# A second-order attention and expert kernel: two block sums left to TensorE, and the row turning, the router and the row load at other places in the batch

## The chip, the cores and the metric

The kernel runs on one core of one Trainium2 chip. The metric is the time of one execution on the device in microseconds (us). The median of three runs before the change is 1181.84 us, from 1178.0 to 1183.53.

## The reference

A layer of attention and a layer of experts, on 8 batches of 512 rows of 256 values, all fp32. Attention uses the second-order Taylor form of the exponential, so a weight is the polynomial 1 + s/4 + s²/32 of the score s; "enc" keys and values come from the first 128 rows of a batch and are seen by all rows.

```python
A_qk = jnp.tril(jnp.einsum('bhnd,bhmd->bhnm', q_f, k_f))      # q_f, k_f: Taylor features
y1 = jnp.einsum('bhnm,bhme->bhne', A_qk, v)
y2 = jnp.einsum('bhnm,bhme->bhne', jnp.einsum('bhnd,bhmd->bhnm', q_f, k_enc_f), v_enc)
k_state = k_enc_f.sum(axis=2, keepdims=True) + jnp.cumsum(k_f, axis=2)
z = 1.0 / ((q_f * k_state).sum(axis=-1) + EPS)                # the denominators
x = _layernorm(x + ((y1 + y2) * z[..., None]) ... @ Wout.T)
# then: 8 experts, each row goes to its best one (router logits x @ wr + br),
# gelu(x @ w1 + b1) @ w2 + b2, times a gate, added to x, and a second layernorm
```

## The kernel before

**Stages.** `attention` runs from the start to about 797 us, `route` (sorting the rows by expert) to about 828 us, and `run_experts` (39 tiles of 128 rows) to the end at 1178.5 us. Only `attention` and its handing over to `route` are touched.

**Pairs, gaps and units.** Attention works through 8 batches b, each of 8 pairs of heads p (n = 8b + p counts them). A pair has four units u: unit 0 is the enc block (512 columns of queries), unit 1 the key block 0 (512), unit 2 the key blocks 3 and 1 (128 + 384), unit 3 the key block 2 (256). A batch has 32 gaps g, one for each unit of each pair: g = 4p + u. In gap g TensorE (PE) makes the scores of unit u of the next pair (`scores(n + 1, u)`, into the PSUM tiles `slot`), weighs the values with unit u of this pair (`weigh(n, u)`, into `osum`), after unit 3 adds up the denominators (`denominators(n)`, into `den`), and then does what a table gives this gap: one *piece*. All pieces go through one PSUM tile, `piece`, so each piece waits (`take_piece`) until another engine has read the one before it. Pieces are the projections of values (`V_LATE_AT` for this batch's second half, `V_EARLY_AT` for the next batch's first half), the projections of queries and keys for the next batch (`QK_AT`), the output projection of the last batch (`OUT_AT`), the turning of its normalised rows (`TURN_AT`) and its router logits (`ROUTER_AT`). The numbers in these tables, `piece_numbers()` and the loops of each engine are all that sets the order; each engine's program is in fixed order.

**Weights.** ScalarE (ACT) squares the scores of a unit into `w`, VectorE (DVE) masks and adds a half (`finish_weights`, L508 and L511). GpSimd (POOL) sums the four key blocks and the enc block of a pair into `wsum`, 512 columns for each of two heads, in five instructions (`add_blocks`: L343, L344, L347, L350, L354), and `denominators(n)` multiplies `wsum` with a column of ones at row p: four matmuls of 256 columns on four 32-column tiles of the array (head s and half c of the queries each have one). `onehot` holds that column. `den` collects 8 pairs; ACT copies it, DVE inverts it at gap 1 of the next batch, SyncE's queue (SP) writes it to `inv_rows` in DRAM (`store_inverse`) and loads it back spread over partitions (`load_inverse`), and DVE multiplies it in (`normalise`, gaps of `NORM_AT`, L520).

**Operands.** Queries and keys of the next batch are split in a high part (ACT, `high_qk`) and a low part (DVE, `low_qk`, L500), written to DRAM by SP (`send(b + 1, m)`: 8 heads for each m, two stores each of `qh`, `ql`, `kh`, `kl`) and gathered back (`gather(b, g)`: `kop` and `qop` of two pairs). `gather(b + 1, 1)`, for pairs 2 and 3, stands in SP's queue behind all of `send(b + 1, 1)`, and so behind the pieces `QK_AT` numbers 3 and 4; PE needs it for the scores of pair 2, at gap 4 of batch b + 1. The projection of queries and keys needs `xl`, the low part of the next batch's input, which DVE makes at gap `XL_GAP` (L492).

**Rows.** `y` holds a batch's input rows (`load_rows`, 512 KB), to which DVE adds the output projection (`residual`), then statistics (`moments`), POOL's `deviation` and DVE's `centre` (L560). SP stores the result, PE turns it (`turn_rows`, L710), ACT copies it to `yT`, PE makes the 8 logits of each row (`router`, L717), and DVE adds the bias (`logits_of`, L565). The next rows may be loaded only when these are turned.

## Time and profile before

| | |
|---|---|
| median of three runs | 1181.84 us |
| the profiled execution: its time, its span | 1180.28 us, 1178.5 us |
| PE busy, of the span | 1063.4 us, 90% |
| DVE, POOL, ACT busy | 634.1, 613.0, 508.0 us |
| last denominators of batches 0 to 7 end at | 117.6, 216.1, 309.1, 402.7, 496.5, 591.5, 684.2, 763.5 us |
| mean granted TensorE clock | 0.95 |

A batch of attention takes 93 to 98 us, the first 117.6 and the last, which projects nothing for a successor, 79.3. The profile is of one execution. Busy time of PE is modelled: matmuls overlap in the pipeline. So stage costs are best read as the distance from the start of one group to the start of the next, and idle time as what stands in square brackets behind a group: how long, and what ended it.

### The profile page before, as it was taken

What the parts mean: (1) busy time and instruction counts of PE and PEld (TensorE: products, weight loads), DVE (VectorE), ACT (ScalarE), POOL (GpSimd) and SP (SyncE); (2) the same over time, 40 slices, a digit from 0 to 9 for tenths busy, and PEclk for the clock granted to TensorE, in tenths of its full rate; (3) what the DMA queues carried; (4) which work ended last, traced back from release to release, by engine and by line L of the source; (5) the groups of instructions that cost most, each with busy time, mean ns of one, the idle gap of its engine ahead of it and who ended that gap; (6) DMA issues with size and microseconds to landing.
All of it is one profiled execution on the core that took longest, in us unless ns stands there. A gap on an engine that the chain in (4) does not pass through costs nothing. (4 is left out here: it accounts for less than half of the span.)

```text
span 1178.5 us, 16833 instructions
## 1 busy us (share of the span) xinstructions
PE 1063.4 (90%) x5296; PEld 621.4 (53%) x5297; DVE 634.1 (54%) x963; ACT 508.0 (43%) x891; POOL 613.0 (52%) x635
## 2 busy tenths in 40 slices
PE   5699899989989989989999998883679999999994
PEld 4344355445445445436545544463357766766763
DVE  5396864683693683585476468447123343333332
ACT  2466644654654663653664464400123233233231
POOL 1397654664673674665576567500134544444442
PEclk9799989999999999999999998995789999999998
DMA  5733631741651552453273261104821011101010
GB/s 208 260 102 106 201 125 64 234 151 41 201 178 69 176 176 97 141 181 126 70 217 122 84 208 59 36 1 197 349 116 33 29 31 34 33 29 33 30 30 1
DMA packets 54111, 134.91 MB, mean 114 GB/s; under 512 B 5854, under 2 KB 10176, under 8 KB 51746
## 3 DMA queue, kind: packets, MB, share of 16 engines
q1 hardware_dynamic: 50306, 124.81, 31.5%
q0 software_dynamic: 3744, 9.31, 2.5%
q8 instruction: 35, 0.57, 0.2%
q14 instruction: 26, 0.21, 0.1%
HBM read 87.73 MB, written 47.29 MB: 115 GB/s over the span
## 5 line engine op out<-in xcount | busy, mean ns | idle before, releaser
L384 ACT ACTIVATE w<-slot 128x1024 f32<-128x1024 f32 (+1 forms) x256 | 231.2, 916 | 176.3 <-PE slot L730 176.1
L751 PE MATMUL osum<-w,values 128*64 128x512 f32 (+3 forms) x1280 | 253.6, 492 | 5.7 <-DVE w L511 5.7
L508 DVE SCALAR_TENSOR_TENSOR w<-w,mask 128x256 f32<-128x256 f32 (+1 forms) x192 | 175.8, 916 | 150.8 <-ACT w L384 138.0
L343 POOL TENSOR_TENSOR wsum<-w 128x512 f32<-128x512 f32 x64 | 95.7, 1496 | 222.7 <-DVE w L511 222.7
L511 DVE TENSOR_SCALAR w<-w 128x768 f32<-128x768 f32 (+2 forms) x192 | 189.4, 986 | 0.0
L347 POOL TENSOR_TENSOR wsum<-wsum,w 128x768 f32<-128x768 f32 x64 | 124.8, 1951 | 60.0 <-DVE w L511 58.2
L1161 ACT ACTIVATE active<-upT,b 128x128 f32<-128x128 f32 x312 | 84.9, 383 | 158.3 <-PE upT L1239 158.3
L1215 PE MATMUL down<-w,active 128*128 x624 | 144.1, 385 | 2.5 <-ACT active L1161 2.5
L1227 PE MATMUL up<-w,rowsT 128*128 x312 | 143.1, 602 | 0.7 <-ACT rowsT L1150 0.7
L730 PE MATMUL slot<-qop,kop 64*128 64x512 f32 (+3 forms) x640 | 126.6, 426 | 9.8 <-issue 7.2
L1215 PEld LDWEIGHTS down<-w,active 128*128 128x128 f32 x624 | 117.5, 193 | 18.6 <-issue 3.8
L730 PEld LDWEIGHTS slot<-qop,kop 64*128 64x128 f32 x640 | 56.2, 188 | 124.3 <-issue 110.5
L674 PE MATMUL piece<-wo,att 128*128 128x256 f32 x448 | 105.5, 389 | 5.7 <-DVE kl L500 5.3
L674 PEld LDWEIGHTS piece<-wo,att 128*128 128x128 f32 x448 | 83.8, 192 | 34.2 <-ACT values L397 9.7
L1192 DVE COPY inner<-up 128x1024 f32<-128x1024 f32 x39 | 47.8, 1225 | 91.7 <-PE up L1227 91.7
L751 PEld LDWEIGHTS osum<-w,values 128*64 128x64 f32 x1280 | 65.4, 136 | 58.5 <-issue 43.3
L344 POOL TENSOR_TENSOR wsum<-w 128x512 f32<-128x512 f32 x64 | 94.1, 1470 | 0.0
L354 POOL TENSOR_TENSOR wsum<-wsum,w 128x512 f32<-128x512 f32 x64 | 86.9, 1358 | 12.2 <-DVE w L511 7.7
L1227 PEld LDWEIGHTS up<-w,rowsT 128*128 128x128 f32 x312 | 57.2, 193 | 58.7 <-issue 58.6
L1175 DVE TENSOR_TENSOR result<-down,b 128x256 f32<-128x256 f32 x39 | 16.6, 425 | 113.5 <-PE down L1215 111.0
L397 ACT ACTIVATE values<-piece 128x512 f32<-128x512 f32 x75 | 44.9, 598 | 75.6 <-PE piece L627 75.5
L389 ACT ACTIVATE w<-w 128x1024 f32<-128x1024 f32 x64 | 67.8, 1060 | 2.0
(187 smaller groups left out, 1210.7 us busy)
## 6 DMA issues: line engine op xcount, KB each, us to landing
kop<-k_rows SPq DMA_DIRECT2D x32, 640.0 KB, 5.8
qop<-q_rows SPq DMA_DIRECT2D x32, 512.0 KB, 7.5
w<-in_w SPq DMA_DIRECT2D x16, 1024.0 KB, 9.3
inv<-inv_rows SPq DMA_DIRECT2D x56, 256.0 KB, 4.5
k_rows<-kh SPq DMA_DIRECT2D x32, 320.0 KB
k_rows<-kl SPq DMA_DIRECT2D x32, 320.0 KB
q_rows<-qh SPq DMA_DIRECT2D x32, 256.0 KB
q_rows<-ql SPq DMA_DIRECT2D x32, 256.0 KB
```

The costliest lines, as they stand in the source:

```text
L343: pool.tensor_tensor(dst[:, 0, :], src[:, 0, 0:N], src[:, 0, N:2 * N], ALU.add)
L344: pool.tensor_tensor(dst[:, 1, :], src[:, 1, 0:N], src[:, 1, N:2 * N], ALU.add).then_inc(wsummed, 1)
L347: pool.tensor_tensor(dst[:, :, P:N], dst[:, :, P:N], src[:, :, 2 * N + P:3 * N], ALU.add).then_inc(wsummed, 1)
L354: pool.tensor_tensor(dst[:, :, 2 * P:N], dst[:, :, 2 * P:N], src[:, :, 3 * N:WIDTH], ALU.add).then_inc(wsummed, 1)
L384: act.activation(w[:, n % 2, :, at:at + cols], slot[u % 2][:, :, 0:cols], ACT.Square, bias=HALF_ROOT).then_inc(squared, 1)
L508: dve.scalar_tensor_tensor(src[:, :, 0:cut], src[:, :, 0:cut], 0.5, mask[:, 0:cut].unsqueeze(1).to_broadcast([P, 2, cut]), ALU.add, ALU.mu ...
L511: dve.tensor_scalar(src[:, :, cut:], src[:, :, cut:], 0.5, None, ALU.add).then_inc(w_ready, 1)
L674: last = pe.matmul(piece[:, 0:D], att[:, (b * PAIRS + p) % ATT, t * P:t * P + P], wo[:, p, :], start=(p == 0), stop=(p == PAIRS - 1))
L730: last = pe.matmul(slot[u % 2][:, s, col:col + N - q0], kop[HD * s:HD * s + HD, n % RING, j * P:j * P + P], qop[HD * s:HD * s + HD, n % RI ...
L751: last = pe.matmul(osum[n % 2][HD * s:HD * s + HD, q0:N], values[:, j, h * HD:h * HD + HD], w[:, n % 2, s, at:at + N - q0], start=(u == 0) ...
L1215: last = pe.matmul(down[k % 2][:, :], active[:, k % 2, c, :], w2[:, bass.ds(e, 1), c, :].rearrange("p o d -> p (o d)"), start=(c == 0), st ...
L1227: last = pe.matmul(up[:, h * 512:(h + 1) * 512], rowsT[:, k % 2, c, :], w1[:, bass.ds(e, 1), c, h * 512:(h + 1) * 512].rearrange("p o d -> ...
```

## The change

- **Denominators.** POOL makes three of its five sums: enc + block 0, and block 1 added to the last 384 columns. Block 2 (256 columns of queries) and the first part of unit 2 (block 3, 128 columns) aren't summed; `denominators` multiplies them straight out of `w`. It becomes 12 matmuls for a pair instead of 4: four of 256, four of 128 and four of 64 columns. For this the halves c are 64 of every 128 columns, not 256 of 512, so `store_inverse` writes runs of 64 values and `spread_inverse` writes strided columns.
- **`square`** waits for the denominators of pair n - 2 in place of its weighing and sums.
- **Turning and router** of batch b's rows move from gaps 26, 28, 30 of batch b + 1 to gaps 7, 9, 10 of batch b + 2. Batch 6 keeps the old places in batch 7.
- **Logits**: ACT copies them out of `piece` and signals it free; DVE adds the bias in SBUF.
- **Tables**: `QK_AT` moves from gaps 10, 12, 14, 25, 27 to 11, 13, 15, 27, 29; `OUT_AT` and `V_EARLY_AT` one gap later, and with them the moments, the deviation and `centre`; one piece of `V_LATE_AT` from gap 5 to 4.
- **Rows**: SP loads `y` behind `gather(b, 3)` in the next batch's queue in place of behind `gather(b + 1, 1)`.

```diff
-RING, ATT, INV = 4, 14, 4
-V_LATE_AT = {0: 0, 1: 1, 3: 2, 5: 3, 6: 4}
-QK_AT = {10: 0, 12: 1, 14: 2, 25: 3, 27: 4}
-OUT_AT = {15: 0, 17: 1, 19: 2, 21: 3}
-V_EARLY_AT = {16: 0, 18: 1, 20: 2, 22: 3, 24: 4}
-TURN_AT, ROUTER_AT = {26: 0, 28: 1}, 30
+RING, ATT, INV = 4, 13, 4
+V_LATE_AT = {0: 0, 1: 1, 3: 2, 4: 3, 6: 4}
+QK_AT = {11: 0, 13: 1, 15: 2, 27: 3, 29: 4}
+OUT_AT = {16: 0, 18: 1, 20: 2, 22: 3}
+V_EARLY_AT = {17: 0, 19: 1, 21: 2, 23: 3, 25: 4}
 XH_GAP, XL_GAP = 7, 8
-NORM_AT = {4: 0, 5: 1, 6: 2, 7: 3, 9: 4, 10: 5, 12: 6, 13: 7}
-INVERT_GAP, MOMENTS_GAP, CENTRE_GAP, RSTD_GAP = 1, 22, 24, 23
+NORM_AT = {4: 0, 5: 1, 6: 2, 7: 3, 9: 4, 10: 5, 11: 6, 13: 7}
+INVERT_GAP, MOMENTS_GAP, CENTRE_GAP, RSTD_GAP = 1, 23, 25, 24
...
+def turned_at(b, g):
+
+    if b >= 2 and g in (7, 9, 10):
+        return [(b - 2,) + {7: ("turn", 0), 9: ("turn", 1), 10: ("router", 0)}[g]]
+    if b == B - 1 and g in (26, 28, 30):
+        return [(b - 1,) + {26: ("turn", 0), 28: ("turn", 1), 30: ("router", 0)}[g]]
+    return []
...
-                        sp.dma_start(inv_rows[PAIRS * s:PAIRS * s + PAIRS, QH * c:QH * c + QH],
-                                     den_sb[at:at + PAIRS, :]).then_inc(inv_out, 16)
+                        rows = inv_rows[PAIRS * s:PAIRS * s + PAIRS, :].rearrange("h (t c n) -> h t c n", c=2, n=64)
+                        sp.dma_start(rows[:, :, c, :], den_sb[at:at + PAIRS, :]).then_inc(inv_out, 16)
...
                 gather(b, 3)
+                if b > 1:
+                    load_rows(b - 1)
                 if b + 1 < B:
                     send(b + 1, 0)
...
                     send(b + 1, 1)
                     gather(b + 1, 1)
-                if b > 0:
-                    load_rows(b)
+            load_rows(B - 1)
...
                 elif u == 2:
-                    pool.wait_ge(wsummed, 4 * n + 1)
+                    pool.wait_ge(wsummed, 2 * n + 1)
                     pool.tensor_tensor(dst[:, :, P:N], dst[:, :, P:N], src[:, :, 2 * N + P:3 * N],
-                                       ALU.add).then_inc(wsummed, 1)
-                    pool.wait_ge(wsummed, 4 * n + 2)
-                    pool.tensor_tensor(dst[:, :, 3 * P:N], dst[:, :, 3 * P:N], src[:, :, 2 * N:2 * N + P],
-                                       ALU.add).then_inc(wsummed, 1)
-                else:
-                    pool.wait_ge(wsummed, 4 * n + 3)
-                    pool.tensor_tensor(dst[:, :, 2 * P:N], dst[:, :, 2 * P:N], src[:, :, 3 * N:WIDTH],
                                        ALU.add).then_inc(wsummed, 1)
...
                 if n >= 2:
-                    act.wait_ge(weighed, UNITS * (n - 2) + u + 1)
-                    act.wait_ge(wsummed, 4 * (n - 1))
+                    act.wait_ge(den_full, n - 1)
...
+            def copy_logits(b):
+                act.wait_ge(piece_full, nth(b, "router", 0) + 1)
+                act.activation(logits[:, bass.ts(b, NT), :], piece[:, 0:NT * E].rearrange("p (t e) -> p t e", e=E),
+                               ACT.Copy).then_inc(raw_copied, 1)
+                act.wait_ge(raw_copied, b + 1)
+                act.sem_inc(piece_read, 1)
...
             def logits_of(b):
-                dve.wait_ge(piece_full, nth(b, "router", 0) + 1)
-                dve.tensor_tensor(logits[:, bass.ts(b, NT), :], piece[:, 0:NT * E].rearrange("p (t e) -> p t e", e=E),
-                                  br[:, :].unsqueeze(1).to_broadcast([P, NT, E]), ALU.add).then_inc(piece_read, 1)
+                dve.wait_ge(raw_copied, b + 1)
+                own = logits[:, bass.ts(b, NT), :]
+                dve.tensor_tensor(own, own, br[:, :].unsqueeze(1).to_broadcast([P, NT, E]), ALU.add)
...
             def denominators(n):
                 b, p = n // PAIRS, n % PAIRS
-                pe.wait_ge(wsummed, 4 * n + 4)
+                pe.wait_ge(wsummed, 2 * n + 2)
...
+                summands = [(0, lambda s: wsum[:, n % 2, s, :]), (2, lambda s: w[:, n % 2, s, 3 * N:WIDTH]),
+                            (3, lambda s: w[:, n % 2, s, 2 * N:2 * N + P])]
+                for k, (t0, src) in enumerate(summands):
+                    for s in range(2):
+                        for c in range(2):
+                            at = 32 * (2 * s + c)
+                            last = pe.matmul(den[at:at + 32, 64 * t0:QH], onehot[:, 31 - p:63 - p],
+                                             src(s).rearrange("p (t c n) -> p t c n", c=2, n=64)[:, :, c, :],
+                                             start=(p == 0 and k == 0), stop=(p == PAIRS - 1 and k == 2),
+                                             tile_position=(0, at), skip_group_check=True)
```

PE before, in batch 3, from unit 2 of gap 10 into gap 12 (`piece<-xh,wqk_h` begins a query or key piece, `slot` is scores, `osum` weighing):

```order
L730 MATMUL slot<-qop,kop 128x128 x2
L730 MATMUL slot<-qop,kop 128x384 x2
L751 MATMUL osum<-w,values 64x128 x2
L751 MATMUL osum<-w,values 64x384 x2
L627 MATMUL piece<-xh,wqk_h 128x512 x2
L627 MATMUL piece<-xl,wqk_h 128x512 x2
L627 MATMUL piece<-xh,wqk_l 128x512 x2
L730 MATMUL slot<-qop,kop 128x256 x2
L751 MATMUL osum<-w,values 64x256 x2
L764 MATMUL den<-wsum,onehot 32x256 x4
L730 MATMUL slot<-qop,kop 128x512 x2
```

PE with the change, at the same place, from unit 2 of gap 10 to the query piece (`piece<-ident,y` would be a turned block, `piece<-wr,yT` is the router):

```order
L722 MATMUL piece<-ident,y 128x128 x4
L742 MATMUL slot<-qop,kop 128x128 x2
L742 MATMUL slot<-qop,kop 128x384 x2
L763 MATMUL osum<-w,values 64x128 x2
L763 MATMUL osum<-w,values 64x384 x2
L729 MATMUL piece<-wr,yT 128x8 x8
L742 MATMUL slot<-qop,kop 128x256 x2
L763 MATMUL osum<-w,values 64x256 x2
L779 MATMUL den<-wsum,onehot 32x256 x4
L779 MATMUL den<-w,onehot 32x128 x4
L779 MATMUL den<-w,onehot 32x64 x4
L638 MATMUL piece<-xh,wqk_h 128x512 x2
```

The query piece stood in gap 10, straight behind the weighing of unit 2; now the router's matmuls stand there, and the query piece comes behind unit 3 and a denominator group of three kinds of matmul.

POOL before, the sums of one pair, and then with the change:

```order
L343 TENSOR_TENSOR wsum<-w 128x512
L344 TENSOR_TENSOR wsum<-w 128x512
L347 TENSOR_TENSOR wsum<-wsum,w 128x2x384
L350 TENSOR_TENSOR wsum<-wsum,w 128x2x128
L354 TENSOR_TENSOR wsum<-wsum,w 128x2x256
```

```order
L350 TENSOR_TENSOR wsum<-w 128x512
L351 TENSOR_TENSOR wsum<-w 128x512
L354 TENSOR_TENSOR wsum<-wsum,w 128x2x384
```

The sums over 2x128 and 2x256 columns are gone.

SP before, between the last operands gathered ahead for a batch and the next batch's own gathers (`inv_rows`: the inverted denominators going out, `inv`: coming back):

```order
L227 DMA kop<-k_rows 128x2x640
L230 DMA qop<-q_rows 128x2x512
L194 DMA y<-in_x 128x1024
L188 DMA xT<-in_xT 128x1024
L242 DMA inv_rows<-den_sb 8x256 x4
L253 DMA inv<-inv_rows 64x1024 x4
L227 DMA kop<-k_rows 128x2x640
L230 DMA qop<-q_rows 128x2x512
L253 DMA inv<-inv_rows 64x1024 x4
L227 DMA kop<-k_rows 128x2x640
```

SP with the change, at the same place, up to the load of the rows:

```order
L233 DMA kop<-k_rows 128x2x640
L236 DMA qop<-q_rows 128x2x512
L194 DMA xT<-in_xT 128x1024
L249 DMA inv_rows<-den_sb 32x1x64 x4
L259 DMA inv<-inv_rows 64x1024 x4
L233 DMA kop<-k_rows 128x2x640
L236 DMA qop<-q_rows 128x2x512
L259 DMA inv<-inv_rows 64x1024 x4
L233 DMA kop<-k_rows 128x2x640
L236 DMA qop<-q_rows 128x2x512
L200 DMA y<-in_x 128x1024
```

The load of `y` no longer follows the gather of `kop` and `qop` that is issued ahead for the next batch; it follows that batch's last gather.

## Rows read from the trace of the kernel before

**Rows 1.** Windows, core 0: stretch, length, busy time by engine (instructions), granted clock, DMA.

```profile
117.50:763.50 646.00, 613.84 (x3344) 321.04 (x3340) 403.85 (x551) 343.21 (x453) 400.28 (x294) 0.98 0.42 135
117.50:216.10 98.60, 92.62 (x494) 48.49 (x490) 61.74 (x82) 50.68 (x67) 59.29 (x44) 0.95 0.42 135
216.10:309.10 93.00, 88.54 (x494) 46.90 (x490) 58.02 (x81) 50.53 (x67) 57.30 (x43) 1.00 0.45 144
```

**Rows 2.** Waits over the whole span: total us, times, longest.

```profile
POOL wsum L343 <- DVE w L511: 222.7, 63, 32.9
...
PE piece L627 <- DVE xl L492: 19.3, 7, 4.9
```

**Rows 3.** PE's timeline, batch 3: start, us, group, [idle before, releaser].

```profile
336.17 0.70 PE L627 MATMUL piece<-xh,wqk_h 128*128 128x512 f32 x2 [3.02 <-DVE xl L492]
...
350.42 3.72 PE L674 MATMUL piece<-wo,att 128*128 128x256 f32 x16 [0.75 <-DVE kl L500]
```

**Rows 4.** Windows again: the stretch behind batch 3's wait for `xl`.

```profile
337.00:340.50 3.50, 3.50 (x18) 1.25 (x16) 3.50 (x4) 1.11 (x2) 3.23 (x2) 0.52 0.16 35
```

**Rows 5.** PE's timeline at full clock, end of batch 2 into batch 3.

```profile
302.15 0.66 PE L710 MATMUL piece<-ident,y 128*128 128x128 f32 x4
...
304.18 0.55 PE L730 MATMUL slot<-qop,kop 64*128 64x128 f32 x4
...
305.68 1.95 PE L717 MATMUL piece<-wr,yT 128*128 128x8 f32 x16
307.56 0.39 PE L730 MATMUL slot<-qop,kop 64*128 64x256 f32 x2
307.87 0.65 PE L751 MATMUL osum<-w,values 128*64 128x256 f32 x4
308.46 0.64 PE L764 MATMUL den<-wsum,onehot 128*32 128x256 f32 x8
309.03 0.50 PE L730 MATMUL slot<-qop,kop 64*128 64x512 f32 x2
309.45 1.08 PE L751 MATMUL osum<-w,values 128*64 128x512 f32 x4
310.46 0.73 PE L627 MATMUL piece<-wv_h,xh 128*128 128x512 f32 x2
```

**Rows 6.** POOL's and DVE's timelines there; POOL's two lines, ns min/median/max.

```profile
309.59 1.83 POOL L347 TENSOR_TENSOR wsum<-wsum,w 128x768 f32<-128x768 f32 x1
...
309.65 1.92 DVE L511 TENSOR_SCALAR w<-w 128x256 f32<-128x256 f32 x1
...
L350 POOL TENSOR_TENSOR wsum<-wsum,w x64: 725/788/1794, 43.0 to 760.7; 128x256 f32<-128x256 f32 x64
...
L354 POOL TENSOR_TENSOR wsum<-wsum,w x64: 1262/1280/1662, 43.8 to 761.5; 128x512 f32<-128x512 f32 x64
```

**Rows 7.** PE's and SP's timelines, batch 3 into 4; DMA issues there, us to landing.

```profile
389.17 0.56 PE L730 MATMUL slot<-qop,kop 64*128 64x128 f32 x4
...
401.24 1.44 SPq L230 DMA_DIRECT2D qop<-q_rows  x1
...
qop<-q_rows SPq DMA_DIRECT2D x1, 512.0 KB, 8.8
...
413.31 0.51 PE L730 MATMUL slot<-qop,kop 64*128 64x512 f32 x2
```

**Rows 8.** PE's timeline, batch 0 into 1.

```profile
107.15 0.55 PE L730 MATMUL slot<-qop,kop 64*128 64x128 f32 x4
...
128.65 0.50 PE L730 MATMUL slot<-qop,kop 64*128 64x512 f32 x2 [0.39 <-DMA qop<-q_rows]
```

**Rows 9.** PE's timeline, the last batch.

```profile
716.91 1.12 PE L751 MATMUL osum<-w,values 128*64 128x256 f32 x4 [1.88 <-DVE w L511]
...
754.49 0.63 PE L710 MATMUL piece<-ident,y 128*128 128x128 f32 x4 [2.37 <-DVE y L560]
```

**Rows 10.** ACT's timeline: a copy of 256 columns out of PSUM.

```profile
309.16 0.39 ACT L436 ACTIVATE den_sb<-den 128x256 f32<-128x256 f32 x1 [0.58 <-PE den L764]
```

More of the change, by code:

```diff
@@ L456, in _ @@
                         copy_values(b + 1, 0, V_EARLY_AT[g - 1])
[L457 to L458 removed]
+                    for owner, kind, k in turned_at(b, g - 1):
+                        if kind == "turn":
+                            copy_turned(owner, k)
+                        else:
+                            copy_logits(owner)
                     if b + 1 < B and g == XH_GAP:
@@ L594, in _ @@
                         residual(b - 1, OUT_AT[g - 1])
-                    if b > 0 and g - 1 == ROUTER_AT:
-                        logits_of(b - 1)
+                    for owner, kind, _ in turned_at(b, g - 1):
+                        if kind == "router":
+                            logits_of(owner)
                     if n < B * PAIRS and u > 0:
@@ L791, in _ @@
                         project_values(b + 1, 0, V_EARLY_AT[g])
-                    if b > 0 and g in TURN_AT:
-                        turn_rows(b - 1, TURN_AT[g])
-                    if b > 0 and g == ROUTER_AT:
-                        router(b - 1)
+                    for owner, kind, k in turned_at(b, g):
+                        if kind == "turn":
+                            turn_rows(owner, k)
+                        else:
+                            router(owner)
             spread_inverse(0)
```

22 lines of the change are left out of this document (7 added, 15 removed).

## The prediction

> **What bounds the kernel now.** I read the windows first [rows 1]. From the end of batch 0's denominators to the end of batch 7's PE is busy 613.84 of 646.00 us, so it idles 32.2 us, and the granted clock there is 0.98: some 13 us went by the half clock (0.02 x 646). DVE, ACT and POOL are busy 404, 343 and 400 us. PE is the bound of attention, and the others count only where PE waits for them. So I read the waits next [rows 2]: POOL's 222.7 us of waiting for DVE cost nothing, PE's 19.3 us in seven waits for `xl` do. The timeline shows the place [rows 3]: gap 10, where the first query piece starts; later in the batch PE waits a second time, 0.75 us, for a key piece's low part. Behind the first of these the clock stands at 0.52, about 1.2 GHz, for 3.5 us [rows 4]; batch 1, where the wait was longest, has a mean of 0.95 and batch 2 has 1.00 [rows 1].
>
> Why is DVE late? At 309.59 POOL starts a sum and ends at 311.42; DVE's addition of a half, started at 309.65, ends at 311.57 [rows 6]. It does nothing while POOL's instruction runs. So POOL's sums cost DVE time, and through it PE.
>
> **Denominators on PE.** Before, a pair's group takes 309.03 - 308.46 = 0.57 us [rows 5]. Added are 192 columns on each of the four array tiles, in eight matmuls (16 instructions, since an fp32 matmul is two). The price of a column: weighing 256 columns of two heads takes 308.46 - 307.87 = 0.59 us, 512 columns 310.46 - 309.45 = 1.01 us, so 0.42 / 256 = 1.64 ns per column where the tiles work beside each other [rows 5]. Lower bound: 192 x 1.64 ns = 0.32 us. Upper bound: each narrower kind also pays the fixed 0.57 - 0.42 = 0.15 us of a group again, 0.62 us. Between them: a weight load of 32 columns belongs to each instruction, and 64 columns give it little cover. The router's matmuls of 8 columns show what a load costs by itself: (307.56 - 305.68) / 16 = 0.117 us for 128 columns [rows 5], so four of 32, one after another, need about as long as a step of 128 columns streams. Taking the 64-column steps as dear as the 128-column ones gives 256 x 1.64 = 0.42, rounded up to 0.43 us, my value. For 64 pairs: **+27.5 us** (20.5 to 40). All of it is on the path, since PE is the bound.
>
> The Trainium skill, page TensorEngine Tiling (Array Packing), section Key Properties, says that different tiles can load weights and multiply in parallel. By it the loads of the four tiles would hide even under 64 columns, and the sum would have 20.5 in place of 27.5; no row here shows tiles under such short streams. It is a rival below.
>
> **POOL's two sums gone.** They take 0.79 and 1.28 us a pair [rows 6], 2.07 us, and nearly all of it is room for DVE in the stretch where DVE is late, three pairs from gap 4 on: some 6 us by gap 16.
>
> **Turning, router and tables.** In batches 2 to 7 two turned blocks (about 0.6 us each; 0.66 us busy) and the router (1.88 us) now stand before the first query piece, and that piece is behind gap 11 instead of 10 (scores, weighing and denominators of unit 3, 309.03 - 307.56 = 1.47 us, plus 0.43) [rows 5]. PE reaches it 3.1 + 1.9 + 0.4 (the earlier pair's denominators) = 5.4 us later, against a wait of 3.02 us [rows 3]. Batch 1 has no turned rows yet and gains only 2.3 us by this, with 2 us or more from POOL's relief, against the longest wait, 4.9 us [rows 2]. So the seven waits go: **-19.3 us**. Of the remaining idle time, 32.2 - 18.2 (six of these waits) = 14.0 us, 2.4 us is a turned block waiting for `centre` in the last batch, and 0.4 us a wait for operands [rows 8, 9]; the rest, 11.2 us, are waits for DVE's low parts and, in the last batch, for weights and sums (1.88 us is the longest) [rows 9]. With 6 us more room for DVE they go: **-11.2 us**. With them goes the half clock, **-13 us**. What would be late next is ACT: it must copy the second turned block within gap 10, where PE scores and weighs for 1.50 us (304.18 to 305.68) [rows 5] and a copy of twice the 256 columns that take 0.39 us [rows 10] fits; I take nothing.
>
> Moving the work costs nothing: batch 1 loses 3.1 us and batch 7 gains it. In batch 7 `centre` is a gap later, but before it waited for POOL, which now is free sooner; the 2.37 us stay.
>
> **The operands for pairs 2 and 3.** Here is the price. Pieces 3 and 4 of `QK_AT` go two gaps later, and the router and turned blocks that stood behind them are gone. Before, from the end of piece 3 (389.17) to the scores that need the gather (413.31) PE worked 24.1 us; the gather's last load, issued at 401.24, landed 8.8 us later, at 410.0, 20.9 us after piece 3 [rows 7]. It had 3.3 us to spare. Now PE's time is 24.1 less two gaps (1.50 for unit 2, 1.47 for unit 3), less two blocks and a router (3.1), plus two denominator groups (0.86): 19.0 us. A chain of 20.9 is 1.9 us late, and PE waits with nothing else in its queue. The rows' load, 512 KB, used to follow the gather and its packets ran beside it; now it is gone from there. That may give back up to 1 us. Against it stands batch 0: no rows' load behind the gather, no turned blocks, and PE did wait, at 128.65, 21.5 us after piece 3 (107.15) [rows 8]. I take 2.5 us after batch 0, 1.2 us for the next five and 0.5 for the last: **+9 us** (0 to 17.5), and **+1.5 us** for a clock that falls once.
>
> **SP's queue.** The rows' load is now between `gather(b, 3)` at gap 11 and the first store of queries, where SP waits for that piece anyhow; it has five gaps, at 1.4 us and a piece each, to land, against the 8.8 us of a load of the same size [rows 7]. `store_inverse` writes runs of 256 bytes instead of 1 KB; a tenth or two later, with DVE's room as cover.
>
> **Logits.** Only the last batch's are on the path, at the head of `route`: an ACT copy, below the 0.39 us of a 256-column copy [rows 10], and one more hand-over, **+0.4 us**.
>
> **Sum.** 27.5 - 19.3 - 11.2 - 13 + 9 + 1.5 + 0.4 = -5.1 us. The profiled execution took 1180.28 us, which gives 1175.2; it lies 1.6 us under the median of the runs, 1181.84, which would give 1176.7. I say **1175 us**.
>
> **The rivals.**
> *The narrow matmuls cost only their columns* (the page's rule): 0.32 a pair, 7 us less, 1168 us. For it: the gap of unit 2, with 128 and 384 columns, takes 1.50 us, and one with 512 in one block 310.46 - 309.03 = 1.43 us, so the split costs 0.07 us [rows 5]. Chance 0.13.
> *The operands land in time*: without the rows' packets the chain is under 19 us, and 10.5 us are saved: 1164.5 us. Against it: batch 0. Chance 0.15.
> *The operands are late as after batch 0, and the clock falls each time*: seven waits of 2.5 us (17.5) and seven stretches of 3.4 us at half clock (7 x 1.7 = 12) instead of 10.5: 1175 + 19 = **1194 us**, slower than before. For it: a wait of 3.02 us did bring the half clock [rows 3, 4]. It makes the kernel slower from some 2.2 us a batch, clock included: 10.5 + 5.1 = 15.6 over seven. Chance 0.12.
> *The upper price of the denominators*: 0.62 a pair, 12 us more, 1187 us. Chance 0.08.
> *The waits for DVE stay*: POOL's sums were not what held it, because DVE starts late at gap 4, for the inverses from DRAM, which now come in smaller runs. Half of the 30.5 us idle and some clock less half of what is saved would give 1175 + 10 to 15, some 1187 us. Against it: PE itself comes 5.4 us later. Chance 0.10.
>
> **How the numbers follow.** My sum, 1169 to 1181, has 0.42. A measurement of this kernel can tell 0.5%, about 6 us: below 1175.9 is faster, above 1187.7 slower. Faster: the two cheap cases (0.28) and over half of my own (0.23), 0.51. Slower: 0.12 and a part of the two at 1187, 0.14. Within: 0.35. The range, 1162 to 1187, leaves out the slow case and the two cheap ones together.
>
> **What the changed profile would show.** The denominator group 1.0 us from its start to the next group (0.89 and 1.19 are the rivals). No PE wait for `xl` or for DVE's low parts. A wait of PE's scores for `qop` at gap 4 of each batch, 1 to 2.5 us. DVE's 256-column addition less often near 1.9 us. Batches 2 to 6 of about 92 to 93 us, batch 1 of about 91. Batches over 95 us, or a PE wait at gap 11, would make me wrong.

## The result and the profile after

The changed kernel took 1196.18 us (median of 4 runs, 1193.95 to 1201.36), the kernel before beside it 1182.22 (4 runs, 1178.0 to 1183.53): ratio 1.0113, 95% interval 1.0073 to 1.0153. It is slower, by 14 us, where 1175 was forecast with a range up to 1187. The profiled execution is the longest of the four, 1201.36 us with a span of 1199.6. Its span is 21.1 us longer than the 1178.5 of before, so the sizes below are those of that execution, and the medians differ by less. In every ratio of this document the runs over 1.5% above the fastest of their kernel are left out; three of the twelve of experiment 8 are such runs, its profiled one among them.

The same windows as in [rows 1], from the end of batch 0's denominators to the end of batch 7's and then three batches:

```profile
116.40:784.50 668.10, 640.34 (x4240) 351.82 (x4236) 371.89 (x551) 346.63 (x460) 280.40 (x181) 0.96 0.41 131
116.40:213.90 97.50, 92.08 (x598) 49.80 (x594) 52.51 (x80) 49.80 (x65) 39.65 (x27) 0.95 0.40 130
213.90:310.30 96.40, 92.67 (x622) 51.26 (x618) 54.29 (x81) 50.98 (x68) 40.22 (x27) 0.98 0.43 137
501.20:600.50 99.30, 95.50 (x618) 52.59 (x618) 54.76 (x81) 51.09 (x68) 40.17 (x27) 0.95 0.43 133
```

The stretch went from 646.00 to 668.10 us, and it holds the whole loss. PE is busy 26.5 us longer (640.34 against 613.84) and idles 27.8 us in place of 32.2. So of the 30 us of waits that were to go most did go, and another wait took their place. The waits of PE say which, beside [rows 2]:

```profile
PE slot L742 <- DMA qop<-q_rows: 17.5, 7, 3.3
...
PE piece L722 <- DVE y L570: 9.2, 2, 5.3
...
PE piece L638 <- DVE ql L510: 6.4, 4, 3.6
```

The scores wait for the query operands after every batch, seven times and 17.5 us in all. PE's timeline at the end of batch 2 and into batch 3, which answers to [rows 5] and [rows 7]:

```profile
300.89 0.73 PE L638 MATMUL piece<-xh,wqk_h 128*128 128x512 f32 x2
...
302.49 0.51 PE L742 MATMUL slot<-qop,kop 64*128 64x512 f32 x2
...
309.36 0.64 PE L779 MATMUL den<-wsum,onehot 128*32 128x256 f32 x8
309.81 0.51 PE L779 MATMUL den<-w,onehot 128*32 128x128 f32 x16
310.26 0.50 PE L742 MATMUL slot<-qop,kop 64*128 64x512 f32 x2
...
320.66 0.63 PE L638 MATMUL piece<-wv_h,xl 128*128 128x512 f32 x2
323.95 0.76 PE L742 MATMUL slot<-qop,kop 64*128 64x512 f32 x2 [2.65 <-DMA qop<-q_rows]
```

Key piece 3 starts at 300.89 and is over at 302.49. The scores that need its gather could begin at 323.95 - 2.65 = 321.30, and begin at 323.95. A pair's denominators take 310.26 - 309.36 = 0.90 us. The window right behind the wait, in the columns of [rows 4]:

```profile
324.10:327.40 3.30, 3.30 (x8) 1.16 (x9) 0.00 (x0) 2.56 (x3) 0.00 (x0) 0.50 0.05 17
```

The clock granted there is 0.50, that is 1.2 GHz, after a wait in which PE did nothing. A stretch at 0.50 follows each of the seven waits, 30.7 us in all, and at half rate that is 15 us lost. In batches 5 and 6, the two of 99 us, there is one more, and no wait stands before it. It comes straight behind the router, whose 16 matmuls are of 8 columns each:

```profile
533.22 1.95 PE L729 MATMUL piece<-wr,yT 128*128 128x8 f32 x16
```
```profile
535.70:539.00 3.30, 3.30 (x31) 1.87 (x28) 3.30 (x3) 0.47 (x1) 2.94 (x2) 0.50 0.67 200
634.70:638.00 3.30, 3.30 (x30) 1.83 (x27) 3.30 (x3) 0.50 (x1) 2.94 (x2) 0.50 0.73 210
```

SP's issues around the wait in batch 3 (start, how long the issue took), and the first multiplication by an inverse on DVE:

```profile
301.38 0.36 SPq L264 DMA_DIRECT2D attention_rows<-y  x1
303.28 1.22 SPq L216 DMA_DIRECT2D q_rows<-qh  x2
...
309.06 2.69 SPq L225 DMA_DIRECT2D k_rows<-kl  x2
311.85 1.69 SPq L233 DMA_DIRECT2D kop<-k_rows  x1
313.59 1.41 SPq L236 DMA_DIRECT2D qop<-q_rows  x1
315.04 1.06 SPq L194 DMA_DIRECT2D xT<-in_xT  x1
317.53 2.81 SPq L249 DMA_DIRECT2D inv_rows<-den_sb  x4
325.96 2.41 SPq L259 DMA_DIRECT2D inv<-inv_rows  x4
```
```profile
330.70 0.69 DVE L530 TENSOR_TENSOR att<-att,inv 128x512 f32<-128x512 f32 x1 [9.20 <-DMA inv<-inv_rows]
```

Three things stand here. The load of the query operands is issued at 313.59 and lands when the wait ends, 10.4 us later. The four stores of the inverses take 2.81 us to issue, and the first load behind them follows 8.4 us after they began. In the kernel before these were 1.30 and 3.25 us in the same batch:

```profile
316.30 1.30 SPq L242 DMA_DIRECT2D inv_rows<-den_sb  x4
319.55 2.42 SPq L253 DMA_DIRECT2D inv<-inv_rows  x4
```

So there are two suspects for the loss, late operands and late inverses.

### The profile page after: what moved, and what is told of

It reads as the page before. It is cut to its first block and busy times, and to the rows that moved or that the text cites. A ratio compares the mean times of both kernels' runs of the same rounds, so it can differ in the third digit from the quotient of the medians.

```text
span 1199.6 us, 18706 instructions
## 1 busy us (share of the span) xinstructions
PE 1090.7 (91%) x6320; PEld 654.8 (55%) x6321; DVE 596.8 (50%) x963; ACT 511.1 (43%) x899; POOL 477.3 (40%) x507
## 5 line engine op out<-in xcount | busy, mean ns | idle before, releaser
L763 PE MATMUL osum<-w,values 128*64 128x512 f32 (+3 forms) x1280 | 258.0, 500 | 0.4 <-DVE w L521 0.3
L518 DVE SCALAR_TENSOR_TENSOR w<-w,mask 128x256 f32<-128x256 f32 (+1 forms) x192 | 141.5, 737 | 154.8 <-ACT w L383 143.2
L521 DVE TENSOR_SCALAR w<-w 128x768 f32<-128x768 f32 (+2 forms) x192 | 170.7, 889 | 0.0
L742 PE MATMUL slot<-qop,kop 64*128 64x512 f32 (+3 forms) x640 | 127.3, 428 | 26.9 <-DMA qop<-q_rows 17.5
L530 DVE TENSOR_TENSOR att<-att,inv 128x512 f32<-128x512 f32 x56 | 38.2, 682 | 63.4 <-DMA inv<-inv_rows 63.4
```

The costliest lines, as they stand in the source:

```text
L518: dve.scalar_tensor_tensor(src[:, :, 0:cut], src[:, :, 0:cut], 0.5, mask[:, 0:cut].unsqueeze(1).to_broadcast([P, 2, cut]), ALU.add, ALU.mu ...
L521: dve.tensor_scalar(src[:, :, cut:], src[:, :, cut:], 0.5, None, ALU.add).then_inc(w_ready, 1)
L742: last = pe.matmul(slot[u % 2][:, s, col:col + N - q0], kop[HD * s:HD * s + HD, n % RING, j * P:j * P + P], qop[HD * s:HD * s + HD, n % RI ...
L763: last = pe.matmul(osum[n % 2][HD * s:HD * s + HD, q0:N], values[:, j, h * HD:h * HD + HD], w[:, n % 2, s, at:at + N - q0], start=(u == 0) ...
```

## The experiments

The lengths are windows from the end of batch 0's denominators to the end of batch 7's, as in [rows 1]. PE's idle time is the length less its busy time; the waits for operands are those of the scores for `qop` at gap 4. Ratios are to the kernel before, run on the same chip as the kernel in question (17 runs of it in the second and third group of kernels, 11 in the first, experiments 1 to 4), with 95% intervals. A profile is one execution, and it need not be the median one.

| kernel | median us | ratio | window | PE busy | PE idle | operands' waits | clock |
|---|---|---|---|---|---|---|---|
| before | 1182.2 | 1 | 646.0 | 613.8 | 32.2 | 0.4 | 0.98 |
| changed | 1196.2 | 1.0113 (1.0073 to 1.0153) | 668.1 | 640.3 | 27.8 | 17.5 | 0.96 |
| pieces 3, 4 earlier | 1193.7 | 1.0114 (1.0075 to 1.0152) | 663.1 | 637.7 | 25.4 | 15.6 | 0.97 |
| denominators alone | 1170.2 | 0.9908 (0.9878 to 0.9939) | 641.3 | 625.0 | 16.3 | none | 0.99 |
| all but the denominators | 1205.1 | 1.0227 (1.0185 to 1.0269) | 670.3 | 624.0 | 46.3 | 18.0 | 0.96 |
| layout alone | 1191.4 | 1.0094 (1.0065 to 1.0124) | 656.0 | 621.7 | 34.3 | 0.3 | 0.96 |
| pieces earlier, y behind | 1166.6 | 0.9874 (0.9844 to 0.9905) | 632.7 | 623.9 | 8.8 | none | 0.99 |
| late half back | 1173.5 | 0.9910 (0.9874 to 0.9946) | 638.6 | 625.9 | 12.7 | none | 0.99 |
| late half back, pieces late | 1190.6 | 1.0055 (1.0026 to 1.0083) | 660.4 | 635.4 | 25.0 | 14.2 | 0.97 |
| denominators, 1 KB runs | 1162.4 | 0.9833 (0.9801 to 0.9864) | 632.8 | 623.0 | 9.8 | none | 0.99 |
| pieces, y behind, 1 KB runs | 1166.1 | 0.9876 (0.9845 to 0.9908) | 631.7 | 623.9 | 7.8 | none | 0.99 |
| y behind alone | 1201.1 | 1.0170 (1.0128 to 1.0211) | 668.8 | 640.6 | 28.2 | 12.8 | 0.96 |
| changed, 1 KB runs | 1199.2 | 1.0147 (1.0116 to 1.0178) | 666.6 | 638.3 | 28.3 | 17.1 | 0.97 |
| pieces, y behind, old denominators | 1177.0 | 0.9977 (0.9954 to 0.9999) | 636.3 | 613.9 | 22.4 | none | 0.98 |

**1. The second send's pieces earlier.** The changed kernel with one line different:

```
-QK_AT = {11: 0, 13: 1, 15: 2, 27: 3, 29: 4}
+QK_AT = {11: 0, 13: 1, 15: 2, 24: 3, 26: 4}
```

> The changed kernel, with the key pieces 3 and 4 of the next batch behind gaps 24 and 26 in place of 27 and 29 (three gaps, about 4.7 us of TensorE's work, earlier), and nothing else. Theory A: the loss is made by late operands. In the changed kernel TensorE waits seven times, 17.5 us in all, for the DMA of the query operands at gap 4, and behind each wait stands a stretch of 3.4 us or more at half clock. Three gaps are more than the longest of these waits (3.3 us), so all seven go, and the clock stretches behind them: 1196 less 17.5 less 7 x 1.7 = 12 gives 1167 us, or up to 1176 if some of the clock is lost elsewhere; mean clock of batches 1 to 7 at 0.97 or more. Rival B: DVE is late for the inverses, whose stores now go in runs of 256 bytes; then the wait moves from the operands to DVE's values and the time stays above 1185 us. Rival C: the pieces, three gaps earlier, themselves wait for DVE's low parts (kl, 0.5 us now), and half of the gain is given back: 1180 us.

1193.7 us, where 1167 to 1176 was expected: a miss. Six waits for the operands remained, 15.6 us. But this run shows where the three gaps went. DVE and SP at the end of batch 2:

```profile
293.66 0.69 DVE L510 SCALAR_TENSOR_TENSOR ql<-piece,qh 128x512 fp32r<-128x512 f32 x1 [5.19 <-ACT qh L408]
...
295.38 3.31 DVE L570 TENSOR_SCALAR y<-y,mv,rstd 128x256 f32<-128x256 f32 x4
```
```profile
298.72 0.36 SPq L264 DMA_DIRECT2D attention_rows<-y  x1
299.19 1.21 SPq L216 DMA_DIRECT2D q_rows<-qh  x2
...
311.37 1.57 SPq L236 DMA_DIRECT2D qop<-q_rows  x1
```

DVE had the piece's low part done at 294.35. SP could not store it, since the store of y stands ahead of the send in SP's queue and waits for the centring at gap 25, which ends at 298.69. With that store only 1.9 us ahead of the send in the changed kernel, the coupling was not visible there: the two moved pieces had been pulled out from behind one wait and straight up against another.

**2. The denominators alone**, in the kernel before: the matmuls of `denominators` as changed, POOL's two sums gone, `cols` and `rows` in views of 64 columns.

```
-                pe.wait_ge(wsummed, 4 * n + 4)
+                pe.wait_ge(wsummed, 2 * n + 2)
+                summands = [(0, lambda s: wsum[:, n % 2, s, :]), (2, lambda s: w[:, n % 2, s, 3 * N:WIDTH]),
+                            (3, lambda s: w[:, n % 2, s, 2 * N:2 * N + P])]
...
-                    pool.wait_ge(wsummed, 4 * n + 2)
-                    pool.tensor_tensor(dst[:, :, 3 * P:N], dst[:, :, 3 * P:N], src[:, :, 2 * N:2 * N + P],
-                                       ALU.add).then_inc(wsummed, 1)
```

> The kernel before with one part of the change alone: two blocks of a pair unsummed to the denominators, POOL's two sums gone, and the layout of 64 columns that this needs; the tables of gaps, the turned rows, the logits and the rows' load stay as before. A pair's denominators took 0.57 us before and 0.90 in the changed kernel, so TensorE gets 64 x 0.33 = 21 us more. Theory A (this part is a plain trade, the loss over it is the tables'): POOL's relief takes away some 10 to 20 us of the 32 us that TensorE idled, so 1182 + 21 less 10 to 20 gives 1183 to 1193 us, and TensorE waits for query operands at gap 4 under 3 us in all. Rival B (the smaller runs of the inverses' stores make DVE late): waits for xl and kl grow, time 1195 us or more.

1170.2 us, faster than either theory had it (1183 to 1193, and 1195 or more). The waits of PE for DVE, where 19.3 us for `xl` stood in [rows 2]:

```profile
PE piece L619 <- DVE xl L484: 8.6, 7, 1.7
...
PE piece L619 <- DVE ql L492: 3.7, 5, 0.8
PE osum L744 <- DVE w L503: 3.4, 4, 1.4
```

It idles 15.9 us less than the kernel before, and none of the waits at gap 10 is over 1.7 us. The added work raised PE's busy time by 11.2 us only, because the clock came up from 0.98 to 0.99. DVE's subtraction that makes `xl`, 1024 columns each time, takes 1.21 us in the median in place of 2.28. So the part of the change that was dear on paper is a gain of 0.9%, and the tables and moves beside it turn that into a loss of 26 us.

**3. All but the denominators.** The changed kernel with five sums on POOL, four matmuls a pair and the old layout; it is the reverse of the diff above.

> The changed kernel with the denominators as in the kernel before (five sums on POOL, four matmuls, the old layout and runs of 1 KB); tables, turned rows and router in gaps 7 to 10, ScalarE's copy of the logits and the rows' load as changed. Theory A: TensorE has 21 us less to do than in the changed kernel, and in the chain from key piece 3 to gap 4 it has two denominator groups less, 0.66 us, so that each wait for the query operands is 0.66 us longer: 7 x 0.66 = 4.6 us, 22 us in all. The waits for xl stay shorter than before (19.3 us) since TensorE comes to the query piece 5 us later: 1196 - 21 + 4.6 + about 5 for DVE, which has POOL's sums against it again, gives 1180 to 1188 us. Rival B: the tables help by themselves and the loss is the denominators' alone: 1170 us or less.

1205.1 us, the slowest of all and past both theories. The waits for the operands are 18.0 us as expected, but those for DVE were put far too low:

```profile
PE piece L646 <- DVE ql L518: 19.3, 6, 4.5
PE slot L749 <- DMA qop<-q_rows: 18.0, 7, 3.3
...
PE den L783 <- POOL wsum L361: 4.5, 4, 2.4
```

The wait at the query piece has not gone, it now carries another name (`ql` in place of `xl`), since DVE is late by as much with POOL's five sums beside it. Taking POOL's sums away is what ended it, not moving the turned rows ahead of it.

**4. The layout alone**, in the kernel before: reads, spread and stores in runs of 64 columns, no other work.

```
-                        sp.dma_start(inv_rows[PAIRS * s:PAIRS * s + PAIRS, QH * c:QH * c + QH],
-                                     den_sb[at:at + PAIRS, :]).then_inc(inv_out, 16)
+                        rows = inv_rows[PAIRS * s:PAIRS * s + PAIRS, :].rearrange("h (t c n) -> h t c n", c=2, n=64)
+                        sp.dma_start(rows[:, :, c, :], den_sb[at:at + PAIRS, :]).then_inc(inv_out, 16)
```

> The kernel before with the layout alone: the denominators' matmuls read four runs of 64 columns of the sums in place of one of 256, the spread matmul writes runs of 64 columns, and the inverses are stored in runs of 256 bytes in place of 1 KB. The work is the same. Theory A: the stores' issue goes from 1.3 to 2.8 us for four on SP and the load behind them comes about 5 us later, once a batch. DVE, which starts the normalising at gap 4, loses part of that, so waits for xl get up to 3 us longer a batch where nothing covers it: 1182 to 1195 us, and the store-to-load time of the trace about 8 us in place of 3.2. Rival B: the smaller runs cost nothing by themselves, the 8.4 us in the changed kernel came from the operands' packets beside them: store to load stays near 3.2 us and the time within 0.3% of 1182.

1191.4 us, 0.9% slower: the inverses do matter in the kernel before. But at the end of batch 2 it is 4.0 us from store to load, where the theory had about 8 and the changed kernel has 8.4. The small runs make the four stores 1.5 us longer to issue, and the load comes 0.8 us later. The waits for `xl` grew from 19.3 to 23.2 us, and PE's busy time by 7.9 us with the same instructions, with the clock at 0.96 in place of 0.98. At full clock a pair's denominators still take 0.57 us, so it is the clock and not the columns' new order that cost PE time: of the 10.0 us by which the window grew 7.9 are the clock and 2.1 idle time.

**5. The earlier pieces, with the store of y behind the send.** Experiment 1 and, in SP's loop:

```
-                if b > 0:
-                    store_rows(b - 1)
                 if b + 1 < B:
                     send(b + 1, 1)
                     gather(b + 1, 1)
+                if b > 0:
+                    store_rows(b - 1)
```

> The changed kernel with key pieces 3 and 4 behind gaps 24 and 26, as in the experiment with the earlier pieces alone, and with the store of y behind the second send and gather in SP's queue in place of ahead of them. In the experiment without the second edit the piece was made at 293.7 us, but its stores stood in SP's queue behind the store of y, which waits for DVE's centring until 298.7, and TensorE waited 15.6 us for the operands in six waits. Theory A: this wait in SP's queue is all that ate the gain of the earlier pieces. Now the stores begin about 5 us earlier, the longest wait was 3.6 us, so all go, with the clock stretches behind them: 1194 less 15.6 less 8 to 12 of clock gives 1166 to 1170 us. Rival B: low parts and operand packets, with the store of y and the next loads beside them, keep the landing late; waits of 1 us or more at gap 4 stay and the time is above 1182 us.

1166.6 us, within the 1166 to 1170 of the theory. No wait for operands is left. SP's issues at the end of batch 2:

```profile
284.72 1.21 SPq L216 DMA_DIRECT2D q_rows<-qh  x2
...
296.69 1.53 SPq L236 DMA_DIRECT2D qop<-q_rows  x1
298.27 0.47 SPq L264 DMA_DIRECT2D attention_rows<-y  x1
```

The send now begins 13.4 us before the end of the batch (298.1 us), where in the changed kernel it began 7.0 us before it (310.3 - 303.28), and before the change 12.8 us (309.1 - 296.31). Its window against that of the changed kernel:

```profile
116.60:749.30 632.70, 623.86 (x4236) 345.43 (x4236) 371.84 (x551) 344.21 (x460) 287.81 (x182) 0.99 0.43 137
```

It is 35.4 us shorter: 19.0 us of idle time, 17.5 of them the operands' waits, and 16.5 us of PE's busy time for the same work. The last is the price of the half clock. Some 15 us of it were lost behind the seven waits, and most of the rest behind the longest wait for `ql`, in batch 1 (3.6 us, where this kernel waits 0.5). Behind the router the half clock came twice here too, in batches 3 and 5.

**6 and 8. The late half of the table back, and then the two pieces late again.** The changed kernel with the gaps of the second half of a batch as before the change; the second run differs from it in one line.

```
-QK_AT = {11: 0, 13: 1, 15: 2, 27: 3, 29: 4}
-OUT_AT = {16: 0, 18: 1, 20: 2, 22: 3}
-V_EARLY_AT = {17: 0, 19: 1, 21: 2, 23: 3, 25: 4}
-INVERT_GAP, MOMENTS_GAP, CENTRE_GAP, RSTD_GAP = 1, 23, 25, 24
+QK_AT = {11: 0, 12: 1, 14: 2, 25: 3, 27: 4}
+OUT_AT = {15: 0, 17: 1, 19: 2, 21: 3}
+V_EARLY_AT = {16: 0, 18: 1, 20: 2, 22: 3, 24: 4}
+INVERT_GAP, MOMENTS_GAP, CENTRE_GAP, RSTD_GAP = 1, 22, 24, 23
```
```
-QK_AT = {11: 0, 12: 1, 14: 2, 25: 3, 27: 4}
+QK_AT = {11: 0, 12: 1, 14: 2, 27: 3, 29: 4}
```

> The changed kernel with the second half of a batch's table as before the change: key pieces 3 and 4 behind gaps 25 and 27, output from 15, values from 16, moments, rstd and centring at 22, 23 and 24 (and, to make room, query pieces 1 and 2 behind 12 and 14). Turned rows and router stay in gaps 7 to 10, as do ScalarE's copy of the logits, the early load of the rows, and the denominators. Theory A: the loss of the changed kernel comes from the late second half, by the operands that it makes late; the early half is sound. No wait for operands at gap 4 (a chain of 20.7 us in 21.9 us of TensorE's work), waits for xl and ql about 5 us in all: 1160 to 1170 us, at or below the 1170 of the kernel with the denominators alone. Rival B: what hurts is the turned rows and router taken from the end of the batch, where they covered the operands' way (3.1 us); then the wait at gap 4 is 1 us or more in most batches and the time above 1180 us.

> The kernel of the late half back, with key pieces 3 and 4 behind gaps 27 and 29 as in the changed kernel, and nothing else. The difference of the two is the price of sending these operands two gaps (3.0 us) later. Theory A: the waits of 1.7 to 3.3 us for the query operands at gap 4 come back in all seven batches, 14 to 19 us, and with each a stretch at half clock, 7 x 1.7 = 12: 20 to 32 us above the kernel of the late half back, 1185 to 1197 us. Rival B: these waits only take over time that is lost anyway (DVE's values are late by as much), so the difference is under 8 us.

1173.5 and 1190.6 us. The first has no wait for operands, though turned rows and router are gone from the end of the batch: rival B of that run falls. It is slower than the 1160 to 1170 of the theory, since PE waits 13.7 us for `ql` in four waits, the longest 5.3, where the second query piece now follows the first by one gap. The second run is the isolated price of sending pieces 3 and 4 two gaps later: 1.0055 - 0.9910 = 1.45%, 17 us, a little under the 20 to 32 expected. Its executions spread widely (1178 to 1206 us), and the profiled one, 1197.56 us, lies 7 us above the median, so its row of the table is rough. Its waits:

```profile
PE slot L742 <- DMA qop<-q_rows: 14.2, 7, 2.9
```

**7, 9 and 11. The inverses in runs of 1 KB.** The rows stay in the order of the denominators' bank, and DVE reads them and `att` through a view. Edited in turn: the kernel with the denominators alone, that of experiment 5, and the changed kernel.

```
-                        rows = inv_rows[PAIRS * s:PAIRS * s + PAIRS, :].rearrange("h (t c n) -> h t c n", c=2, n=64)
-                        sp.dma_start(rows[:, :, c, :], den_sb[at:at + PAIRS, :]).then_inc(inv_out, 16)
+                        sp.dma_start(inv_rows[PAIRS * s:PAIRS * s + PAIRS, QH * c:QH * c + QH],
+                                     den_sb[at:at + PAIRS, :]).then_inc(inv_out, 16)
...
-                dve.tensor_tensor(att[:, n % ATT, :], att[:, n % ATT, :], inv[:, n % INV, :],
-                                  ALU.mult).then_inc(normalised, 1)
+                own = att[:, n % ATT, :].rearrange("p (t c n) -> p c t n", c=2, n=64)
+                dve.tensor_tensor(own, own, inv[:, n % INV, :].rearrange("p (c t n) -> p c t n", c=2, n=64),
+                                  ALU.mult).then_inc(normalised, 1)
```

> The kernel with the denominators alone (1170.2 us), where the inverses are kept in the order of the denominators' bank: they are stored in runs of 1 KB again, and DVE's multiplication reads the broadcast inverses and the att tile through a view of runs of 64. Theory A: small runs cost 4.0 us from store to load in place of 3.2, and 2.8 us of issue on SP in place of 1.3; DVE gets the inverses 1 to 2 us earlier, which takes some of the 8.6 us of waits for xl: 1164 to 1170 us. Rival B: nothing waits on it any more, 1170 within 2 us. If the multiplication by runs of 64 takes longer than 0.68 us, 1172 or more.

> The two best edits together: the changed kernel with key pieces 3 and 4 behind gaps 24 and 26, the store of y behind the second send in SP's queue, and the inverses stored in the order of the denominators' bank in runs of 1 KB. Theory A (inverses 1.7 us earlier on DVE, 7 to 8 us saved where the denominators stood alone): in the kernel with y behind, 6 to 7 us of waits for ql and kl are left, some of which go; 1160 to 1165 us. Rival B: the turned rows have already taken TensorE past DVE's late stretch, the inverses bind nothing there, and the time stays 1166.6 within 2 us.

> The changed kernel with the inverses stored in runs of 1 KB as its only edit. In it the inverses took 8.4 us from their store to their load in a queue behind the operands' packets. Theory A: the wait for the operands at gap 4 sets the time and is untouched, so little comes of it: 1190 to 1196 us, with 15 us or more of waits for the query operands. Rival B: the small packets are what holds the operands' own packets up; then the waits at gap 4 shrink by 1 us or more each, and the time is under 1185 us.

Where the denominators stand alone, the runs of 1 KB bring 1170.2 to 1162.4 us, a little below the 1164 to 1170 of the theory and the fastest median of the study. SP's stores and first load, small runs first, then those of 1 KB:

```profile
311.39 2.81 SPq L243 DMA_DIRECT2D inv_rows<-den_sb  x4
315.42 2.41 SPq L253 DMA_DIRECT2D inv<-inv_rows  x4
```
```profile
314.17 1.30 SPq L242 DMA_DIRECT2D inv_rows<-den_sb  x4
316.54 2.41 SPq L253 DMA_DIRECT2D inv<-inv_rows  x4
```

From store to load it is 2.4 us in place of 4.0, and the waits for `xl` fell from 8.6 us in seven waits to 3.5 in three. DVE's multiplication takes 679 ns with either view (median of 56). The Trainium skill, page DMA: Bandwidth & Descriptors, section Specifications, gives 512 bytes as the least transfer for line rate; this case agrees in direction, with 4.0 us from store to load for runs of 256 bytes against 2.4 for 1 KB, but no run here measures the rate.

In the kernel of experiment 5 the same edit does nothing (1166.1 against 1166.6; the theory had 1160 to 1165), as its rival B had it: the inverses bind nothing there. PE's waits for `ql`, `kl` and `w` are 7.5 us with the edit and 7.2 without. In the changed kernel it does nothing either, 1199.2 against 1196.2 with intervals that overlap; the theory had 1190 to 1196. The stores and the load there:

```profile
318.29 1.50 SPq L248 DMA_DIRECT2D inv_rows<-den_sb  x4
326.68 2.42 SPq L259 DMA_DIRECT2D inv<-inv_rows  x4
```

With runs of 1 KB it is still 8.4 us. So that delay was not made by small runs. It goes with the late operands: at the end of every batch where PE waits for operands it is 6.2 to 9.7 us, in this kernel, the changed one and experiments 1, 3, 8 and 10; in all the other kernels it is 2.3 to 5.6 us. In the changed kernel the stores at 317.53 stand behind the operands' load and behind the load of `xT`, issued at 315.04, which took 10.1 us to land and so was there at 325.1; the first load of the inverses is issued at 325.96.

**10. The store of y behind the send, and nothing else**, in the changed kernel; the diff is that of experiment 5.

> The changed kernel with the store of y behind the second send in SP's queue as its only edit; key pieces 3 and 4 stay behind gaps 27 and 29. With the three kernels that exist (changed; pieces earlier; pieces earlier and y behind) it closes a table of two by two. Theory A: in the changed kernel the store of y was issued 1.9 us before the second send's first store, so it is not what that send waits for; the waits at gap 4 stay and the time is 1196 within 4 us. Rival B: the packets of y's 512 KB, just ahead of the send, are what slows it; then the waits at gap 4 lose 1 us or more each and the time is under 1188 us.

1201.1 us, just above the 1192 to 1200 of the theory, with an interval that overlaps the changed kernel's. The waits for operands are 12.8 us, 4.7 less, but the time did not follow; those for `ql` are 10.2 in place of 6.4. The table of two by two is then: y ahead, 1196.2 with the pieces late and 1193.7 early; y behind, 1201.1 late and 1166.6 early. Neither edit is worth anything alone, both together 30 us.

**12. Experiment 5 with the old denominators.** Both diffs are above.

> The kernel with pieces 3 and 4 behind gaps 24 and 26 and the store of y behind the second send, with the denominators as in the kernel before (all five sums on POOL, four matmuls, runs of 1 KB). It shows what the tables are worth without the denominators' part, once the operands are in time. Theory A: TensorE has 21 us less to do than in the run with y behind (1166.6), but POOL's sums hold DVE, and the waits for ql, kl, w and wsum (30 us in the run of the tables alone) stay: 1165 to 1180 us. Rival B: with the operands in time the waits for DVE go too, since they followed from the same lateness, and the 21 us come in full: 1150 us or less.

1177.0 us, within the theory's range, and faster than the kernel before by no more than 0.5%. PE waits 17.0 us for `ql` in seven waits and 5.1 for POOL's sums. Against experiment 5 the denominators on PE are worth 1.0% (0.9977 to 0.9874), as they were against the kernel before (1 to 0.9908), although they add 21 us to the engine that is the bound.

## Why the prediction was wrong

The prediction named its own sign of failure, batches over 95 us: batches 2 to 6 are 96.4, 95.8, 95.1, 99.3 and 99.0 us long.

**The operands' wait, with its clock, was the step that failed.** The mechanism, the place and the rival were there: "The operands are late as after batch 0, and the clock falls each time", 1194 us, with a chance of 0.12. PE's work between piece 3 and the scores was put at 19.0 us (its terms add up to 18.9) and is 321.30 - 302.49 = 18.8. The chain was put at 20.9 us, of which the rows' load, now gone from beside it, "may give back up to 1 us". It took 323.95 - 302.49 = 21.5 us, the very length of the one wait that was in the trace, after batch 0 [rows 8]. That batch was read as an exception, and it was the one example without the rows' load. Its 21.5 less 19.0, seven times, is 17.5 us, the measured total, where 9 stood in the sum; that it fits to the tenth is luck, for the single waits are from 1.7 to 3.3 us. That rival's 1194 us is near the median for a mixed reason too: its denominators were 6.5 us too dear and its other waits 10 us too few. Experiment 8 against 6 shows the cause, and experiment 5 that its removal gives back 30 us.

**The clock was given back, then taken again.** The sum had -13 us for the half clock that would go, and +1.5 for one fall. In the window PE's busy time grew 26.5 us, of which the denominators are 56 x 0.33 = 18.5; so the clock cost 8 us more than before, not 11.5 less. This is the largest single error of the sum, and most of it follows from the operands: one fall was forecast, and seven came, worth 15 us. Of the others, the two behind the router have no wait to explain them. Together the terms of operands and clock missed by 8.5 + 19.5 = 28 us; the sum was 26 below the profiled execution (1175.2 against 1201.36) and 21 below the median. The two terms that follow, 6.5 us too much and some 10 too little, in part cancel.

**The denominators were cheaper than the value taken.** 0.90 - 0.57 = 0.33 us a pair, 21 us in all, in place of 0.43 and 27.5. This is the lower bound, 192 columns at the price of a column, and the rival with 0.13. The Trainium skill, page TensorEngine Tiling (Array Packing), section Key Properties, says that different tiles can load weights and multiply in parallel; this trace agrees, with 0.33 us measured where the prediction's lower bound, a price by columns alone, was 0.32.

**The waits for `xl` went as forecast, with exceptions.** Of 19.3 us 5.8 are left, now mostly under the name `ql`: 1.7 in batch 0, 3.6 in batch 1, 0.5 in batch 2. But experiment 3 shows that the reason given first was the weaker one: with PE arriving later and POOL's sums in place the waits stay, 19.3 us in six, and experiment 12, without late operands, has 17.0 in seven. POOL's relief, costed as "room for DVE", does the most by itself (8.6 us left in experiment 2, with the clock at 0.99).

**The other waits did not all go.** Of 11.2 us some 4 are left: 0.5 to 0.7 us for low parts or a projection in four batches, and the turned block in the last batch waits 3.9 us for the centring in place of 2.4. That "the 2.37 us stay" was wrong, since the centring is a gap later: with it, and the output before it, a gap earlier in experiment 6, this wait is gone.

**The inverses**: "a tenth or two later" was wrong by much, 5 us (8.4 against 3.25), and DVE's first multiplication by an inverse comes 20.4 us after the end of the batch (330.70 against 310.3). No run takes this delay away and nothing else; experiment 11 left it at 8.4 us. But it can have cost little: in experiment 5, where it is 4.0 us, PE waits 7.2 us for `ql`, `kl` and `w`, against 8.3 us in the changed kernel. Its part by small runs, 0.8 to 1.6 us, shows in the time only where PE comes to the query piece early: 8 us in experiment 7, 11 us in experiment 4.

**SP's queue** was walked through for the rows' load and not for the store of y. In the changed kernel that cost nothing; it hid the remedy in experiment 1.

**What stays open**: what makes the clock fall behind one wait, or one router, and not behind the next of the same length, and why SP needs 1.22 us to issue two stores of a piece at 303.28 and 2.69 us at 309.06, with the packets of the pieces ahead still under way.

## What to carry to other kernels

Where a table delays the start of a long chain of stores and loads, take the chain's length from the only place where something already waited for it, even if that place looks special, and multiply by the number of batches; a wait of some 2.5 us a batch was paid here once in idle time (17.5 us) and nearly once more in clock (15 us). Work may be worth putting on the bound engine when it frees the engine that the bound one waits for: 21 us more on TensorE made this kernel 0.9% faster, and 1.7% with the inverses in runs of 1 KB. And when an earlier start brings nothing, look at what stands ahead of it in the same queue before giving the theory up: two edits worth nothing alone were worth 2.4% together.

## What was not expected of the hardware

The clock does not fall behind every wait. In the changed kernel it fell behind all seven for operands, of 1.7 to 3.3 us; in experiment 2 it stayed up behind the six waits for `xl` of 1.0 to 1.7 us in batches 1 to 6, and in experiment 8 behind waits for operands of 0.9, 1.6, 1.6 and 1.9 us. The middle is wide. In the kernel before it stayed up behind the waits for `xl` of 2.3 and 2.0 us, and in experiment 3 behind one of 3.3 us for the operands, at 715.11:

```profile
242.50:246.00 3.50, 3.50 (x24) 1.79 (x24) 3.50 (x5) 1.08 (x2) 2.78 (x2) 1.00 0.39 91
```
```profile
715.20:718.60 3.40, 3.40 (x16) 1.55 (x16) 0.00 (x0) 2.92 (x4) 0.00 (x0) 1.00 0.42 111
```

In batches 1 to 6 of all the runs it fell behind no wait under 1.7 us and behind every one over 3.45; between the two both were seen. So a forecast can price the long waits with their clock and the short ones without it, and has to leave the middle open.

Nor does it need a wait. In batches 3 to 7 of experiment 12 it fell within 1.7 us behind the router each time, and in experiment 5 twice, in batches 3 and 5, where PE had no idle time over 0.3 us for 75 us and more. The router's piece is 1.9 us of matmuls of 8 columns. A kernel with such a piece can lose some of its clock there, and nothing in its waits will say so.

The clock also tells executions of one kernel apart. The fastest of the twelve of experiment 12, 1169.8 us, had a mean granted clock of 0.950, the slowest, 1185.56 us, 0.937, with the same instructions.

A queue of stores can stand behind data that is not its own: from four small stores of 8 KB to the next load it took 2.3 to 5.6 us in the runs whose operands were in time, and 6.2 to 9.0 us in the changed kernel; with runs of 1 KB in place of 256 bytes it was 6.8 to 9.7 there.
